# Splitting a weight load into eight queue events in an order-planned transformer kernel

## The reference

```python
x = x + attn_a(layernorm(x))   # 16 heads of 16, causal softmax over 1024 keys, W1 (256 x 768), Wp (256 x 256)
x = x + ffn(layernorm(x))      # silu(x wg) * (x wu), then wd; integer weights / 127, hidden 768
x = x + attn_b(layernorm(x))   # 16 heads of 16, sliding window of 64 keys, 63 given keys and values ahead
x = x + ffn(layernorm(x))      # the same weights as above
```

## Time and profile before

| what | value |
|---|---|
| median of 3 runs | 1445.09 us (1439.43 to 1447.42) |
| the profiled execution's own time | 1449.58 us |
| its span, first to last instruction | 1447.9 us |
| PE busy | 1264.0 us, 87% |
| DVE busy | 916.2 us, 63% |
| ACT busy | 780.0 us, 54% |
| mean granted TensorE clock | 0.958 of full |

### The profile page before, as it was taken

How to read it: one execution, slowest core, us unless ns; L and a number is a source line. 1 busy time by engine, 2 the same in 40 slices (tenths; PEclk the granted TensorE clock), 3 DMA queues, 4 the chain that set the end, 5 groups by cost and what they waited for, 6 DMA issues and landing times.

```text
span 1447.9 us, 25167 instructions
## 1 busy us (share of the span) xinstructions
PE 1264.0 (87%) x9601; PEld 823.4 (57%) x9601; DVE 916.2 (63%) x1628; ACT 780.0 (54%) x1122; POOL 394.5 (27%) x383
## 2 busy tenths in 40 slices
PE   2588988997998998997899998899789899899887
PEld 2453337865873335875685333786577433487566
DVE  4478845575768873566477884547566887356643
ACT  2246584554445667454654667455554566755453
POOL 2222223311434213311333222331133421331132
PEclk9999999998999999999899999899999999999989
DMA  7630111433233021253135011143323402125310
GB/s 292 200 109 17 51 69 60 121 95 120 103 105 111 25 89 31 85 151 127 57 107 162 18 48 72 59 121 95 119 103 96 120 21 93 31 68 164 128 35 30
DMA packets 103513, 134.20 MB, mean 93 GB/s; under 512 B 29057, under 2 KB 88769, under 8 KB 100161
## 3 DMA queue, kind: packets, MB, share of 16 engines
q1 hardware_dynamic: 103392, 132.57, 29.4%
HBM read 51.45 MB, written 11.61 MB: 44 GB/s over the span
## 4 chain that ended last, share of the span: by engine, by line
PE 62%; ACT 11%; DVE 7%; SPq 7%; DMA 6%; issue 4%; POOL 1%; POOLq 0%; ACTq 0%; DVEq 0%
PE ring L1310 11%; PE ring L1282 9%; PE ring L1260 8%; PE ring L1347 6%; PE ring L1348 6%; SPq L1535 6%; PE ring L1236 5%; ACT probs_causal L1087 4%; PE ring L1362 4%; DMA q_st<-peak_b 3%; PE ring L1367 3%; DVE peak L842 3%; ACT L1026 3%; PE ring L1201 2%; PE ring L1202 2%
## 5 line engine op out<-in xcount | busy, mean ns | idle before, releaser
L842 DVE TENSOR_REDUCE peak<-ring 128x1 f32<-128x640 f32 (+5 forms) x480 | 461.0, 1005 | 95.3 <-PE ring L1236 93.6
L1087 ACT ACTIVATE probs_causal<-ring 128x1024 f32<-128x1024 f32 (+1 forms) x320 | 288.5, 939 | 159.5 <-PE ring L1282 143.2
L1282 PE MATMUL ring<-q_st,k_st 98*128 98x512 bf16 (+5 forms) x1408 | 240.4, 290 | 45.7 <-DMA q_st<-peak_b 33.7
L1260 PE MATMUL ring<-k_st,q_st 96*128 96x192 bf16 (+4 forms) x1280 | 242.3, 298 | 32.3 <-ACT probs_causal L1087 10.7
L1282 PEld LDWEIGHTS ring<-q_st,k_st 98*128 98x128 bf16 (+1 forms) x1408 | 107.7, 101 | 179.1 <-ACT probs_causal L1087 44.5
L1347 PE MATMUL ring<-xt_hi,w_gu_sb 128*128 128x512 f32 x384 | 161.5, 421 | 18.8 <-DVE xt_lo L816 18.8
L772 POOL TENSOR_SCALAR_AFFINE_SELECT probs_causal<-probs_causal 128x512 f32<-128x512 f32 x128 | 81.4, 636 | 352.7 <-ACT probs_causal L1087 352.6
L1260 PEld LDWEIGHTS ring<-k_st,q_st 96*128 96x128 bf16 x1280 | 98.8, 97 | 131.2 <-ACT probs_causal L1087 40.5
L784 POOL TENSOR_TENSOR h_lo<-hid,h_hi 128x512 fp32r<-128x512 f32 x96 | 126.7, 1330 | 167.1 <-ACT h_hi L1137 166.6
L1310 PE MATMUL ring<-probs_causal,V 128*32 128x512 f32 (+3 forms) x1536 | 165.6, 507 | 6.4 <-ACT probs_causal L1087 4.4
L778 POOL TENSOR_TENSOR onf<-onf,o_hi 128x512 fp32r<-128x512 f32 x64 | 83.4, 1308 | 283.9 <-ACT o_hi L1107 283.6
(11 more groups left out here) (115 smaller groups left out, 1961.2 us busy)
## 6 DMA issues: line engine op xcount, KB each, us to landing
q_st<-q_part SPq DMA_DIRECT2D x192, 128.0 KB, 2.4
w_gu_sb<-img_gu SPq DMA_DIRECT2D x16, 1536.0 KB, 8.7
k_st<-k_part SPq DMA_DIRECT2D x144, 128.0 KB, 2.4
w_qkv<-img_qkv SPq DMA_DIRECT2D x8, 1536.0 KB, 6.4
on_hi<-o_hi SPq DMA_DIRECT2D x64, 128.0 KB, 2.7
on_lo<-onf SPq DMA_DIRECT2D x64, 128.0 KB, 2.8
k_st<-k_part SPq DMA_DIRECT2D x48, 144.0 KB, 2.5
x_next<-in_x SPq DMA_DIRECT2D x4, 1024.0 KB, 5.7
```

The costliest lines, as they stand in the source:

```text
L842: dve.tensor_reduce(dst, heads_of(flat_of(a, e), unit, plan.a_width(i)), AX.X, ALU.max).then_inc(a_max, 1)
L1087: act.activation(block[0:rows, n % slots, h:h + heads, 0:w], heads_of(flat_of(a, e), unit, w)[0:rows], ACT.Exp).then_inc(exp_done, 1)
L1260: pe.matmul(psum[:, per * n + c:per * n + c + d], q, keys[0:SP_ROWS, head, first_key + c:first_key + c + d], start=(per * n % 512 == 0), s ...
L1282: last = pe.matmul(psum[0:rows, per * n:per * n + w], keys[:, head, first_key:first_key + rows], queries[:, head, q0 - HALF * hf:q1 - HALF ...
```

## The change

The gate and up weights are loaded in eight transfers of 768 words a partition (384 KB) in place of two of 3072 words. Each is an event of its own, with a like of its own (`D`, in place of `F`). In the planner's costs, all load events now hold SP for the time of their bytes (1.4 us for a piece, 4.2 for `qkv`, 3.3 for `x`, 1.8 for `wp` and `store`), and their result is there 2.3 us later. Both sets of `LIKES` are replaced, so all events are ordered anew. Four pieces count up the semaphore of the first part and four that of the second, and the waits take the new counts; what each wait is for stays the same. The planner lets the first G start only when the last piece is there, while the program's wait is for the first part.

```diff
+PIECES = 8
 LIKES = (
-    dict(turn=0.06, ahead0=3.35, ahead1=0.51, lead0=1.28, lead1=8.78, late=-0.49, Q=1.95, q=4, S=1.09, E=-0.74,
-         P=0.93, A0=2.55, A1=0.83, N0=0.35, N1=1, T0=1.6, T1=0.91, B0=0.58, B1=0.56, V0=0.65, V1=0.49, C0=1.39,
-         C1=0.23, R0=0.25, R1=0.45, ..., F=1.18, ...),
-    dict(turn=0.75, ahead0=-1.14, ahead1=2.98, lead0=1.8, lead1=-1.51, late=2.58, Q=-0.73, q=-1.53, S=-1.15,
-         E=1.38, P=-0.49, A0=-0.81, A1=0.4, N0=-1.11, N1=-1.36, T0=-0.02, T1=2.36, ..., C1=-1.04,
-         R0=-1.06, R1=0.18, ..., F=1.42, ...))
+    dict(turn=-0.43, ahead0=-0.31, ahead1=0.83, lead0=1.56, lead1=1.46, late=0.46, Q=-0.18, q=0.52, S=-3.7,
+         E=-3.54, P=-1.08, A0=-0.51, A1=-0.17, N0=-0.18, N1=0.66, T0=-0.23, T1=0.15, B0=-0.74, B1=-0.2, V0=-0.95,
+         V1=-0.83, C0=-0.71, C1=-0.76, R0=-0.45, R1=0.33, ..., F=0.17, D=3.46, ...),
+    dict(turn=3.06, ahead0=-0.87, ahead1=-0.46, lead0=2.17, lead1=2.22, late=-3.43, Q=0.2, q=-1.36, S=-1.94,
+         E=4.95, P=0.16, A0=1.1, A1=-1.2, N0=-3.04, N1=-2.28, T0=-1.32, T1=-1.66, ..., C1=-1.62,
+         R0=-1.08, R1=-1.61, ..., F=2.25, D=-1.78, ...))
...
-               [("F", "wp")], [("F", "gu", 0), ("F", "gu", 1)]]
+               [("F", "wp")], [("F", "gu", n) for n in range(PIECES)]]
...
-            return [("SP", 0.6, {"wp": 3.0, "gu": 6.0, "qkv": 6.0, "store": 4.0, "x": 4.0}[e[1]])]
+            return [("SP", {"wp": 1.8, "gu": 1.4, "qkv": 4.2, "store": 1.8, "x": 3.3}[e[1]], 2.3)]
...
+        if e[:2] == ("F", "gu"):
+            return "D"
...
-            turned = [(("L", 2 + k // 6), 2), (("F", "gu", 1), 0)] if own else []
+            turned = [(("L", 2 + k // 6), 2), (("F", "gu", PIECES - 1), 0)] if own else []
...
-                    pe.wait_ge(gu_in[0], 16 * (a + 1))
+                    pe.wait_ge(gu_in[0], 8 * PIECES * (a + 1))
...
-                    sp.wait_ge(gu_in[1], 16 * a)
+                    sp.wait_ge(gu_in[1], 8 * PIECES * a)
...
-                    sp.dma_start(w_gu_sb[a % 2][:, n, :, :].rearrange("p k c -> p (k c)").bitcast(F32),
-                                 img_gu[:, 3072 * n:3072 * n + 3072]).then_inc(gu_in[n], 16)
+                    c = slice(6144 // PIECES * n, 6144 // PIECES * (n + 1))
+                    sp.dma_start(w_gu_sb[a % 2][:].rearrange("p g k c -> p (g k c)")[:, c].bitcast(F32),
+                                 img_gu[:, c]).then_inc(gu_in[2 * n // PIECES], 16)
```

More of the change, by code:

```diff
@@ L55 @@
 LIKES = (
-    dict(turn=0.06, ahead0=3.35, ahead1=0.51, lead0=1.28, lead1=8.78, late=-0.49, Q=1.95, q=4, S=1.09, E=-0.74,
-         P=0.93, A0=2.55, A1=0.83, N0=0.35, N1=1, T0=1.6, T1=0.91, B0=0.58, B1=0.56, V0=0.65, V1=0.49, C0=1.39,
-         C1=0.23, R0=0.25, R1=0.45, M0=0.34, M1=-1.05, H0=0.73, H1=-0.16, K0=2.58, K1=2.53, O=0, Y=-0.24, W=0.39,
-         Z=1.2, L=2.39, G=-2.84, I=-0.77, J=-2.53, F=1.18, g=1.94, i=1.73, j=2.01, w=2.95, x=-2.62, k=-2.47,
-         X=0.98),
-    dict(turn=0.75, ahead0=-1.14, ahead1=2.98, lead0=1.8, lead1=-1.51, late=2.58, Q=-0.73, q=-1.53, S=-1.15,
[L62 to L65, removed]
+    dict(turn=-0.43, ahead0=-0.31, ahead1=0.83, lead0=1.56, lead1=1.46, late=0.46, Q=-0.18, q=0.52, S=-3.7,
+         E=-3.54, P=-1.08, A0=-0.51, A1=-0.17, N0=-0.18, N1=0.66, T0=-0.23, T1=0.15, B0=-0.74, B1=-0.2, V0=-0.95,
+         V1=-0.83, C0=-0.71, C1=-0.76, R0=-0.45, R1=0.33, M0=-0.65, M1=-2.83, H0=-1.14, H1=0.25, K0=-0.81,
+         K1=0.04, O=0.51, Y=-2.46, W=-1.17, Z=-0.82, L=0.98, G=-0.36, I=-4.18, J=0.92, F=0.17, D=3.46, g=0.07,
+         i=0.05, j=1.98, w=0.18, x=1.68, k=3.03, X=-0.98),
+    dict(turn=3.06, ahead0=-0.87, ahead1=-0.46, lead0=2.17, lead1=2.22, late=-3.43, Q=0.2, q=-1.36, S=-1.94,
+         E=4.95, P=0.16, A0=1.1, A1=-1.2, N0=-3.04, N1=-2.28, T0=-1.32, T1=-1.66, B0=-2.47, B1=-2.29, V0=0.49,
+         V1=0.59, C0=0.25, C1=-1.62, R0=-1.08, R1=-1.61, M0=-2.9, M1=-3.91, H0=1.06, H1=1.52, K0=2.15, K1=-2.67,
+         O=-3.59, Y=-3.16, W=-2.34, Z=2.65, L=0.76, G=-3.85, I=-4.51, J=-1.57, F=2.25, D=-1.78, g=0.55, i=2.39,
+         j=0.12, w=2.57, x=2.75, k=-0.51, X=0.73))
 def running(counts):
@@ L1337, in gate_up @@
                 if k == 0:
-                    pe.wait_ge(gu_in[0], 16 * (a + 1))
+                    pe.wait_ge(gu_in[0], 8 * PIECES * (a + 1))
                     if wide_weights:
-                        pe.wait_ge(gu_in[1], 16 * (a + 1))
+                        pe.wait_ge(gu_in[1], 8 * PIECES * (a + 1))
                 pe.wait_ge(xlo_done, 4 * a + 3 + h)
```

## The result

The changed kernel takes 1390.46 us (median of 4 runs, 1384.36 to 1395.92) against 1444.09 for the kernel before, a ratio of 0.963 with an interval of 0.9598 to 0.9661: 3.7% faster, 53.6 us. The forecast was 1417 with a range of 1391 to 1450. The sign was right and the size was half of what came. The time lies 0.5 us outside the range.

The account below looks back on a forecast made before the run. PE was taken to set the pace (62% of the chain), with 183.9 us idle to win from. Terms −27.1 + 3.8 − 6.0 + 3.8 − 2.8 = −28.3 us, 1.95% off the 1445.1 median, gave 1417, range 1391 to 1450.

Parts of the forecast that it names:

- The gap: Sliding layers: PE's idle 6.65 to 6.91 us ahead of group 6's first B goes, −27.1 us over four layers.
- one piece ahead: Sliding layers: one piece still goes ahead of group 6's maxima, +3.8 us over four layers, bounds 0 to 7.5.
- the next transfers: Sliding layers: group 7's maxima and group 6's sums now may have a piece ahead, +3.8 us, bounds 0 and 7.5.
- the clock: Sliding layers: PE's lowered clock behind the gap goes, −6.0 us over four layers, bounds 0 and −7.6.
- The forecast of transfers that overlap in the queue: SP's queue: fixed parts of transfers overlap, so a piece costs 0.94 us, not the skill's estimated 2.9.
- The causal term: Layers 2, 4 and 6: PE loses 0.94 us each on group 5's sums behind the load; −2.8 us.
- All else ordered anew: All layers: the new order of all other events, taken at 0, bound 3 us a layer, 24 us, either way.
- Rival 1: The order itself pays: A far enough ahead that several waits for maxima shrink, 3 us a layer, 1393; chance 0.14.
- Rival 4: Causal layers: A held back leaves the maxima's journeys bare before B, 47 us slower, 1464; chance 0.20.
- Rival 2: Sliding layers: maxima of group 6 or 7 still stand behind most of the pieces, 1439; chance 0.13.
- The signs that I had named: No line 1282 gap over 2 us, 64 issues with maxima between, clock 1.00, sliding layers 6 to 8 us shorter, causal within 3.

Follow-up runs that it names:

- g: Kernel before, old order; in the sliding layers eight pieces spread among maxima, sums and packed parts: 1418.6 us, ratio 0.9824.
- h: Kernel before, old order; in the sliding layers the two whole transfers moved behind group 7's maxima: 1412.9 us, ratio 0.9788.
- a: Kernel before, old order; each of the two gate and up transfers issued as four pieces in the old place: 1457.4 us, ratio 1.008.
- p: Changed kernel's causal order, old sliding order with two transfers behind group 7's maxima as in h: 1398.2 us, ratio 0.9689.
- l: Changed kernel's causal order, old sliding order with eight pieces spread as in g: 1398.2 us, ratio 0.9686.
- m: Changed kernel, but in the sliding layers the load goes as two transfers behind group 6's sums: 1388.1 us, ratio 0.9627.
- j: As h, and in three causal layers SP sends group 1's maxima two stack events earlier: 1412.3 us, ratio 0.9792.
- b: Kernel before, old order; in the sliding layers the two transfers moved right behind group 6's maxima: 1443.6 us, ratio 1.0001.
- n: As b, with group 7's maxima put ahead of group 5's reciprocal on DVE and SP: 1439.2 us, ratio 0.9959.
- i: Changed kernel, but in the sliding layers the load goes as two transfers behind group 7's maxima: 1412.2 us, ratio 0.9778.

## Why the prediction was off, point by point

- *The gap, −27.1, with one piece ahead, +3.8, and the next transfers, +3.8; the clock, −6.0.* Right as a sum, within the noise. Without the causal term it is −25.5; kernel g, which is this part alone, measured −25.4 (18 to 33), and h, another way to it, −30.6. That g meets the sum to 0.1 us is luck. In detail, the changed kernel has no piece ahead of group 6's maxima and three ahead of group 7's, with no gap at either in layer 3, so both terms of +3.8 came at their lower bound there; the clock is at 1.00 through both windows.
- *The forecast of transfers that overlap in the queue* held: six more transfers cost 1.1 us (a). The Trainium skill's page "DMA: Bandwidth & Descriptors", section "Anatomy of one DMA — SWDGE (gpsimd) path", gives some 2.0 us fixed for each DMA on GpSimd's path; added up for six more transfers this would be an estimated 12 us. On SP's queue here the trace doesn't agree with such a sum: it shows the 1.1.
- *The causal term, −2.8, for the sums of group 5.* Not shown by itself. The changed kernel has all eight pieces ahead of these sums in a causal layer, and DVE doesn't wait for them: in its new order the passes of group 7 and its maxima come ahead of the reciprocal, which then starts at 517.63 with no idle time before it. So what such a wait costs is not in the bytes alone, but in what is queued behind it.
- *"All else ordered anew", taken at 0.* This is the step that failed: a term of the sum that was put at nothing and came to some 23 to 28 of the 53.6 us (what is left beyond h's 30.6 and g's 25.4). The new causal order has 14 (h to p) to 20 us (g to l) of it, and the new sliding order 8 (l to the changed kernel) to 9 (p to m). My bound of 3 us a layer, 24 in all, was about as large as the term; with it the low end was 1393, and the range reached to 1391.
- *Rival 1, the order pays as well,* at 0.14, had the number right. Its mechanism, waits for maxima that shrink, is not what the runs show for the most part: outside the four large gaps PE waited 6.6 us for maxima before (33.7 in all, less 27.1) and waits 3.5 now, and kernel j, which took away three such waits, gained nothing clear.
- *Where the order gains* is settled only in part. The cleanest pair is g and l, which have the same sliding plans: their causal stretches are 201.2, 201.8 and 201.5 us against 194.6, 193.9 and 194.8, and PE idles 17.8, 17.3 and 17.1 us in them against 12.1 in each. The window of layer 2's stretch in the changed kernel is

```profile
365.00:563.00 198.00, 184.72 (x1257) 102.63 (x1256) 139.33 (x229) 118.88 (x159) 60.63 (x62) 0.97 0.26 77
```

and PE idles 13.3 us (198 − 184.7) where it idled 17.6 before (202 − 184.45 in 379 to 581 us). Two of the gaps of before are gone, both in the first groups:

```profile
410.60 0.38 PE L1260 MATMUL ring<-k_st,q_st 96*128 96x128 bf16 x4 [1.76 <-DVE xt_lo L816]
...
447.90 1.36 PE L1282 MATMUL ring<-q_st,k_st 98*128 98x512 bf16 x6 [1.99 <-DMA q_st<-peak_b]
```

Together they are 3.75 us, beside a net 4.3, and the second lies in the stretch with the mean clock of 0.86 (it is at 0.50 from 450 to 453). Kernel j speaks against the maxima's place on SP as the cause by itself. Which of the many moved steps it is stays open.
- *Rival 4, slower, with A held back:* it didn't come. DVE is busy with its passes for 10.21 and 10.61 of 12 us in layer 2's first groups, and in the whole kernel PE waits for maxima three times, 3.5 us together.
- *Rival 2, the wait that moves,* didn't come in the changed kernel, but it came in b, n and i. I had put its price at 22 us (20 + 6 − 4). It was 22 in i against the changed kernel, and 25 in n and 31 in b against h.
- *The signs that I had named.* The gap at line 1282, the 64 issues with maxima between them, and the clock came as said. The stretches did not: sliding ones 9.4 to 11.4 us shorter and not 6 to 8, causal ones 3.2 to 4.3 shorter, where I had said within 3. Both are signs of a gain beyond the load's.

## What to carry to other kernels

When one large load shares a queue with small transfers, list the next four or five of them with what waits for each, and place the load behind the last one that something urgent is queued behind; moving it by one place may only hand the wait to the next in line. Splitting helps only if the pieces are truly put between the others, and costs some issue time otherwise. And where a change replaces a whole order, the new order deserves a term of its own with both signs: here it was worth about as much (23 to 28 us) as the defect that the trace showed (25 to 31). And don't read from a stretch of one layer kind what its own plan is worth, when the plan can pass work on to the next.

## What the runs showed of the hardware

A transfer issued 1 to 2 us behind the 3 MB took 9.7 to 9.8 us until what waited for it could go on, with 8 KB in b and i (9.71 and 9.70) as with 128 KB in n (9.78, the third transfer behind the block). And eight issues in a row held SP 3.66 to 5.03 us in the eight layers of kernel a, where two took 0.82 to 1.00 in the kernel before.
